# Powers ahead of other work on GpSimd, one operation for each tile's router score, and the gather split among output products

## The chip, the cores and the metric

The kernel runs on one core of one Trainium2 chip. The metric is the device time of one execution in microseconds (us); what is compared is the median of several executions.

## What is computed

One transformer layer without learned scales: attention with shared keys and values, a layer norm, a feed-forward network that only half of the rows pass through, and another layer norm. Cut to what matters:

```python
# x: (2, 512, 256) float32
k = x @ W_lat + b_lat                                  # one key and value of width 128 for all heads
q = (x @ W_d + b_d).reshape(2, 512, 16, 128)           # 16 heads
att = softmax(causal(q @ k.T / sqrt(128)))
y = (att @ k).reshape(2, 512, 16 * 128)
x1 = layernorm(x + y @ W_proj + b_proj)

scores = x1 @ router_weight + router_bias              # (2, 512)
top_scores, indices = top_k(scores, 256)               # half of the rows of each batch
selected = x1[indices]
h = gelu(selected @ w1 + b1)                           # 1024 wide
weighted = (h @ w2 + b2) * sigmoid(top_scores)
out = layernorm(x1 with weighted added at the selected rows)
```

## The kernel before

All work is laid out by hand: each engine has its own list of instructions, in a fixed order, and semaphores carry the dependencies. Products run in a split form: a float32 operand is cut into a rounded high part and a low part (what the rounding left), and `product` (L387) issues three matmuls, high by high, high by low and low by high. Whoever needs a product therefore waits for a high part (a cast, mostly on ACT) and a low part (a subtraction, on DVE or POOL).

**Attention.** There are 32 units, 16 heads of two batches, and a software pipeline over periods: in a period PE computes the scores of one unit, turns the probabilities of the unit before (`turn`, L473, three groups of exact transposes) and multiplies them with the values (`values`, L528), and adds the unit before that into the output projection (`project`, L505). For the turned probabilities ACT writes `pT_last` and `pT_hi` (`turned`, L723) and DVE writes `pT_lo` (`turned`, L891). Batch 0's norm, router and ranking are cut into pieces and put into single periods of batch 1's attention (`middle_piece`, L952, and `last_piece`, L982, on DVE, by the period numbers of L284).

**Router.** For each of four tiles of 128 rows `router_dots` (L1066) sums (row - mean) * weight into `dots` on DVE. POOL raises the variance to the power -1/2 (`inverse_deviation`, L1308), in two halves of two tiles; the variance was multiplied by 0.25 before (L1052), so this `rstd` is twice the true one, and all rows of x1 are kept doubled. `router_scores` (L1075) multiplies `dots` by `rstd` for the four tiles at once into `dots_scaled`, and then by 0.5 plus the bias into `score`. PE turns each tile's score column into a row, the same on all partitions (`turn_scores`, L547). `compare` (L1085) counts on DVE for each row whom it beats, PE sums the columns (`rank_cols`, L553), `losses` (L1102) and `ranks` (L1107) make the rank of each row. Batch 0's rows are scattered to DRAM by rank and read back; batch 1's are also gathered by PE, with a matrix of zeros and ones `sel` (`select`, L1114; `gather`, L573).

**After attention** nothing but batch 1's router chain and both networks is left. The order of each engine around the change is:
- PE (L669 to L679): the last hidden products of batch 0, two of the eight output products of rows 0 (`net_out(0, 0, ...)`), `turn_scores(1)`, the other six, `rank_cols(1)`, three products of rows 1, all of `gather`, five products, the hidden layer of batch 1, and its output products for rows 0 and rows 1. In `net_out` the argument f runs over eight slices of the hidden width; a slice is one `product`, three matmuls.
- DVE (L1148 to L1172): norm statistics, aggregates and variances of the two halves (`ps_out` holds the rows), four `router_dots`, `router_scores`, `layernorm_apply` of tiles 0 and 1, four `compare`, `losses`, `gates`, `layernorm_apply` of tiles 2 and 3, `ranks`, `select` of tiles 0 and 1, a low part, `select` of tiles 2 and 3, `layernorm_stats` of the four tiles, `chosen_low` (the low part of the gathered rows, which the hidden layer of batch 1 waits for), aggregates, variances, and `add_up` of batch 0. Then the low parts of batch 1's hidden layer (`hidden_low`, L1174), with norm work between them.
- POOL (L1357 to L1373): `hidden_low` (L1351) for the eight slices of batch 0, with the first power ahead of slice 3 and the second ahead of slice 4; `x1_low(0)` (L1315), the four scatters of `push(1)`, powers, the two scatters of batch 0's chosen rows (`put_back`, L1342), and then for each of batch 1's two row groups a power (L1371) and its scatter.
- ACT: gelu and casts; `row_of_scores(1)` (L787), `x1_high` (L782) and `chosen` (L813) come between the two hidden layers.
- SP: loads and stores, `store_all(0)`, `load_picked(1)`, `store_all(1)` (L377 to L380).

The two score operations, as they stand before:

```python
dve.tensor_tensor(dots_scaled[:, b, :], dots[:, b, :], rstd[:, b, :],
                  ALU.mult).then_inc(dots_scaled_done[b], 1)
dve.wait_ge(dots_scaled_done[b], 1)
dve.tensor_scalar(score[:, b, :], dots_scaled[:, b, :], 0.5, rb_all[:, 0:1],
                  ALU.mult, ALU.add).then_inc(score_done[b], 1)
```

## Time and profile before

| what | value |
|---|---|
| median of 3 runs | 287.74 us (287.42 to 287.77) |
| the profiled execution's own time | 287.92 us |
| its span, first to last instruction | 286.2 us |
| granted clock of PE, mean | 0.995 |
| PE busy | 275.0 us, 96% of the span |
| DVE busy | 220.6 us, 77% |
| ACT busy | 208.2 us, 73% |
| POOL busy | 155.5 us, 54% |

The span is counted from the start of the first instruction; 1.7 us of the execution's time lie around it. All points of time below are microseconds from the start of the span. Attention ends at about 253.7; the rest is the tail of the kernel. The chain of waits is the list of what ended last, step by step; the timelines list the instructions of one engine with their start and duration, and in brackets the idle time before one and who ended it. Instructions of an engine overlap a little: the next one starts some 0.08 us before the end of the one in front on DVE, and matmuls are pipelined.

### The profile page before, as it was taken

What the parts mean: (1) busy time and instruction counts of PE and PEld (TensorE: products, weight loads), DVE (VectorE), ACT (ScalarE), POOL (GpSimd) and SP (SyncE); (2) the same over time, 40 slices, a digit from 0 to 9 for tenths busy, and PEclk for the clock granted to TensorE, in tenths of its full rate; (3) what the DMA queues carried; (4) which work ended last, traced back from release to release, by engine and by line L of the source; (5) the groups of instructions that cost most, each with busy time, mean ns of one, the idle gap of its engine ahead of it and who ended that gap; (6) DMA issues with size and microseconds to landing.
All of it is one profiled execution on the core that took longest, in us unless ns stands there. A gap on an engine that the chain in (4) does not pass through costs nothing.

```text
span 286.2 us, 6205 instructions
## 1 busy us (share of the span) xinstructions
PE 275.0 (96%) x1886; PEld 249.1 (87%) x1886; DVE 220.6 (77%) x698; ACT 208.2 (73%) x571; POOL 155.5 (54%) x215
## 2 busy tenths in 40 slices
PE   7998999999999999999999999999999999998990
PEld 4777999999999999999999999998999999897990
DVE  2588777777777777777888888899978987679782
ACT  3588778777777777888897777788777777863540
POOL 3737743333333346555556756666668664257543
PEclk9999999999999999999999999999999999999998
DMA  5582111111111111111111111111112210020331
GB/s 186 128 293 76 53 32 33 33 36 37 37 37 37 37 37 40 37 37 41 37 37 39 37 40 37 38 39 37 40 38 76 58 36 2 1 76 0 99 124 37
DMA packets 18842, 15.53 MB, mean 54 GB/s; under 512 B 1641, under 2 KB 18178, under 8 KB 18818
## 3 DMA queue, kind: packets, MB, share of 16 engines
q1 hardware_dynamic: 18242, 13.65, 16.4%
q0 software_dynamic: 576, 1.58, 1.6%
q8 instruction: 12, 0.20, 0.3%
q14 instruction: 12, 0.10, 0.1%
HBM read 12.60 MB, written 2.63 MB: 53 GB/s over the span
## 4 chain that ended last, share of the span: by engine, by line
PE 83%; DVE 7%; ACT 3%; issue 2%; POOL 2%; SPq 1%; DMA 1%; POOLq 0%; DVEq 0%; ACTq 0%
PE bank L390 18%; PE bank L392 17%; PE bank L391 16%; PE bank L491 8%; PE ps_out L390 6%; PE ps_out L392 6%; PE ps_out L391 6%; PE bank L544 2%; PE bank L469 2%; DVE hid_lo L1177 1%; DMA bias_rows<-in_L_ffn_b 1%; DVE beats L1098 1%; DVE x_row L1063 1%; DVE st L1036 1%; PE bank L581 0%
## 5 line engine op out<-in xcount | busy, mean ns | idle before, releaser
L720 ACT ACTIVATE probs<-probs,negmax 128x512 f32<-128x512 f32 (+3 forms) x128 | 72.6, 575 | 6.5 <-DVE negmax L887 5.1
L1230 POOL TENSOR_TENSOR wd_hi<-wd_raw,zero 128x256 fp32r<-128x256 f32 x32 | 24.7, 772 | 92.3 <-DVE probs L948 87.5
L727 ACT CAST pT_hi<-bank 128x512 fp32r<-128x512 f32 (+2 forms) x96 | 43.5, 488 | 28.6 <-PE bank L491 28.6
L887 DVE CUSTOM_DVE_ANT_0 probs<-bank,mask_row 128x512 f32<-128x512 f32 (+3 forms) x128 | 59.1, 482 | 0.6 <-PE bank L392 0.6
L894 DVE TENSOR_TENSOR pT_lo<-bank,pT_hi 128x512 fp32r<-128x512 f32 (+2 forms) x96 | 53.0, 553 | 7.4 <-ACT pT_hi L727 6.8
L491 PEld LDWEIGHTS bank<-ident_r,prob_words 128*128 128x128 f32 x320 | 34.2, 140 | 5.6 <-issue 0.2
L390 PE MATMUL bank<-kT_hi,qT_hi 128*128 128x512 f32 (+2 forms) x96 | 37.3, 388 | 0.2 <-DVE qT_lo L841 0.2
L390 PE MATMUL ps_out<-wp_hi,yT_hi 128*128 128x256 f32 x124 | 37.2, 300 | 0.0
L392 PE MATMUL ps_out<-wp_hi,yT_lo 128*128 128x256 f32 x124 | 35.0, 282 | 0.0
L491 PE MATMUL bank<-ident_r,prob_words 128*128 128x128 f32 x320 | 35.0, 240 | 0.0
L391 PE MATMUL ps_out<-wp_lo,yT_hi 128*128 128x256 f32 x124 | 35.0, 282 | 0.0
L390 PE MATMUL bank<-pT_hi,k_hi 128*128 128x512 f32 (+2 forms) x96 | 32.9, 342 | 1.1 <-DVE pT_lo L894 1.1
L905 DVE TENSOR_TENSOR yT_lo<-bank,yT_hi 128x512 fp32r<-128x512 f32 x31 | 21.4, 690 | 16.2 <-PE bank L392 12.3
L392 PE MATMUL bank<-kT_hi,qT_lo 128*128 128x512 f32 (+2 forms) x96 | 32.6, 340 | 0.0
L391 PE MATMUL bank<-pT_lo,k_hi 128*128 128x512 f32 (+2 forms) x96 | 32.4, 337 | 0.0
L391 PE MATMUL bank<-kT_lo,qT_hi 128*128 128x512 f32 (+2 forms) x96 | 32.4, 337 | 0.0
L392 PE MATMUL bank<-pT_hi,k_lo 128*128 128x512 f32 (+2 forms) x96 | 32.2, 335 | 0.0
L948 DVE TENSOR_SCALAR probs<-probs,rinv 128x384 f32<-128x384 f32 (+2 forms) x96 | 28.7, 356 | 1.1
L769 ACT ACTIVATE probs<-probs,rinv 128x512 f32<-128x512 f32 x32 | 23.2, 724 | 8.2 <-DVE rinv L942 8.2
L1230 POOL TENSOR_TENSOR wp_hi<-wp_raw,zero 128x256 fp32r<-128x256 f32 x32 | 23.5, 736 | 10.2 <-DVE probs L948 10.2
L841 DVE SCALAR_TENSOR_TENSOR qT_lo<-bank,bias_cols,qT_hi 128x384 fp32r<-128x384 f32 x32 | 19.7, 617 | 11.8 <-ACT qT_hi L690 11.2
L390 PE MATMUL bank<-xT_hi,wd_hi 128*128 128x512 f32 x64 | 27.8, 434 | 0.1
(168 smaller groups left out, 728.7 us busy)
## 6 DMA issues: line engine op xcount, KB each, us to landing
wd_raw<-in_L_attn_W_d SPq DMA_DIRECT2D x32, 128.0 KB, 2.2
wp_raw<-in_L_attn_W_proj SPq DMA_DIRECT2D x32, 128.0 KB, 2.1
wf_raw<-in_L_ffn_w SPq DMA_DIRECT2D x2, 1024.0 KB, 7.1
x_nat<-in_L_attn_x SPq DMA_DIRECT2D x4, 256.0 KB, 2.9
out<-z_all SPq DMA_DIRECT2D x4, 256.0 KB, 2.2
picked<-ranked SPq DMA_DIRECT2D x2, 258.0 KB, 3.1
wlat_raw<-in_L_attn_W_lat SPq DMA_DIRECT2D x1, 128.0 KB, 3.5
bproj_all<-in_L_attn_b_proj SPq DMA_DIRECT2D x1, 128.0 KB, 3.4
```

The source lines that it names most:

```text
L390: pe.matmul(dst, lh, rh, start=first, stop=False, skip_group_check=check)
L391: pe.matmul(dst, lh, rl, start=False, stop=False, skip_group_check=check)
L392: return pe.matmul(dst, ll, rh, start=False, stop=last, skip_group_check=check)
L491: last = pe.transpose(dst[:, a:a + P].bitcast(F32R), prob_words[s][:, P_OFF[j] + i * P:P_OFF[j] + (i + 1) * P], ident_r[:, :])
L720: act.activation(p_tile(s, j), p_tile(s, j), ACT.Exp, bias=negmax[:, s, j:j + 1], scale=-1.0, accum_out=sums[:, s, j:j + 1]).then_inc(exp_ ...
L727: act.copy(pT_hi[:, turns[n][3]], turns[n][2]).then_inc(pt_hi_done, 1)
L769: act.mul(p_tile(at.place(0), 3), p_tile(at.place(0), 3), rinv[:, at.place(0), 3:4]).then_inc(norm_act, 1)
L887: dve.tensor_tensor_reduce(p_tile(s, j), score_bank[j], mask_row[:, (TILES - 1 - j) * P:], -SCALE, -MASKED, ALU.add, ALU.min, accum_out=ne ...
L894: dve.tensor_tensor(pT_lo[:, dst], src, pT_hi[:, dst].bitcast(F32), ALU.subtract).then_inc(pt_lo_done, 1)
L905: dve.tensor_tensor(y_lo[:, :], ps_y[:, :], y_hi[:, :].bitcast(F32), ALU.subtract).then_inc(y_lo_done, 1)
L948: dve.tensor_scalar(p_tile(s, j), p_tile(s, j), rinv[:, s, j:j + 1], None, ALU.mult).then_inc(norm_dve, 1)
L1230: pool.tensor_tensor(hi, src, nothing, ALU.add).then_inc(hi_done, 1)
```

## The change

- POOL: batch 1's second power comes right behind its first, ahead of `hidden_low(3)`; at the end both powers come ahead of both scatters of batch 1.
- DVE: the router's weight row is halved once, in period 16 (`rw_half`), and used by `router_dots`; `router_scores` becomes four operations of one column each, with two scalars per partition (`rstd` and the bias), and each counts up `score_done`.
- PE: `turn_scores` waits for one tile's score at a time and is an exact transpose of 32-bit words (the float32r form, as for the probabilities) instead of a float32 one. `gather` is cut in two halves: four products of rows 1, half the gather, one product, the other half, three products.
- In the last values period (at.fixed == UNITS, period 32) `pT_last` is copied by DVE behind its `pT_lo`, no longer by ACT ahead of `pT_hi`.
- DVE: the norm statistics of tiles 2 and 3 of batch 1 move behind `chosen_low`.

```diff
+        words = ExitStack()
+        score = sb("score", [P, BATCH, TILES], F32, words)
+        words.close()
+        score_words = sb("score_words", [P, BATCH, TILES], F32R)
+        rw_half = sb("rw_half", [P, DIM])
...
             def turn_scores(b, dst):
-                pe.wait_ge(score_done[b], 1)
                 for j in range(TILES):
-                    last = pe.transpose(dst[:, j * P:(j + 1) * P], score[:, b, j:j + 1].to_broadcast([P, P]), ident[:, :])
+                    pe.wait_ge(score_done[b], j + 1)
+                    last = pe.transpose(dst[:, j * P:(j + 1) * P].bitcast(F32R),
+                                        score_words[:, b, j:j + 1].to_broadcast([P, P]), ident_r[:, :])
...
-            def gather():
+            def gather(half):
-                pe.wait_ge(gelu_done[0], FCH)
-                for j in range(TILES):
+                if half == 0:
+                    pe.wait_ge(gelu_done[0], FCH)
+                for j in (2 * half, 2 * half + 1):
...
             rank_cols(1, ps_t1)
-            net_out(0, 1, range(0, 3))
-            gather()
-            net_out(0, 1, range(3, FCH))
+            net_out(0, 1, range(0, 4))
+            gather(0)
+            net_out(0, 1, range(4, 5))
+            gather(1)
+            net_out(0, 1, range(5, FCH))
...
             def turned(at, n):
                 wait(act, pt_ready, at.p * 3 - 2 + n)
-                if n == 2:
+                if n == 2 and at.fixed != UNITS:
                     act.copy(pT_last[:, :], ps_t0[:, 0:P]).then_inc(pt_last_done, 1)
...
             def turned(at, n):
+                if n == 2 and at.fixed == UNITS:
+                    wait(dve, y_ready, UNITS - 1)
+                    dve.tensor_copy(pT_last[:, :], ps_t0[:, 0:P]).then_inc(pt_last_done, 1)
...
             def last_piece(at):
+                if at.fixed == AT_OUT - 1:
+                    dve.wait_ge(rows_in, 64)
+                    dve.tensor_scalar(rw_half[:, :], rw_all[:, :], 0.5, None, ALU.mult).then_inc(rw_halved, 1)
...
             def router_dots(b, tiles):
-                if b == 0:
-                    dve.wait_ge(consts, CONSTS)
+                dve.wait_ge(rw_halved, 1)
...
-                                             rw_all[:, :], ALU.subtract, ALU.mult,
+                                             rw_half[:, :], ALU.subtract, ALU.mult,
...
-                dve.tensor_tensor(dots_scaled[:, b, :], dots[:, b, :], rstd[:, b, :],
-                                  ALU.mult).then_inc(dots_scaled_done[b], 1)
-                dve.wait_ge(dots_scaled_done[b], 1)
-                dve.tensor_scalar(score[:, b, :], dots_scaled[:, b, :], 0.5, rb_all[:, 0:1],
-                                  ALU.mult, ALU.add).then_inc(score_done[b], 1)
+                for j in range(TILES):
+                    dve.tensor_scalar(score[:, b, j:j + 1], dots[:, b, j:j + 1], rstd[:, b, j:j + 1], rb_all[:, 0:1],
+                                      ALU.mult, ALU.add).then_inc(score_done[b], 1)
...
             def compare(b, tiles):
+                dve.wait_ge(score_done[b], TILES)
...
-            layernorm_stats(1, 1, range(TILES))
+            layernorm_stats(1, 1, (0, 1))
             chosen_low()
+            layernorm_stats(1, 1, (2, 3))
...
             for f in range(FCH):
-                if f in (3, 4):
-                    inverse_deviation(1, 0, f - 3)
+                if f == 3:
+                    for half in range(2):
+                        inverse_deviation(1, 0, half)
                 hidden_low(f)
...
             for r in range(RCH):
                 pool.wait_ge(last_var_done, r + 1)
                 pool.tensor_tensor(rstd[:, 2 * BATCH + 1, r:r + 1], ve[:, 2 * BATCH + 1, r:r + 1],
                                    minus_half[:, r:r + 1], ALU.pow).then_inc(rstd_done[1], 1)
+            for r in range(RCH):
                 put_back(1, r)
```

## Rows read from the trace of the kernel before

**Rows 1.** Chain of waits, head 31's values: start us, us, what.
```profile
248.90 0.15 ACT pT_last L726
...
249.84 0.39 PE bank L390
```

**Rows 2.** Chain of waits, PE at batch 0's score turn.
```profile
186.28 0.44 PE bank L550 x4
...
187.95 0.56 PE bank L491 x7
```

**Rows 3.** Timeline of DVE, batch 1's scores: start us, us, instruction, [idle before].
```profile
255.27 0.17 DVE L1052 TENSOR_SCALAR ve<-mv 128x2 f32<-128x2 f32 x1
...
256.97 0.08 DVE L1071 DVE_READ_ACCUMULATOR squared<-ps_out,mv,rw_all 128x1 f32 x1
257.65 0.62 DVE L1079 TENSOR_TENSOR dots_scaled<-dots,rstd 128x4 f32<-128x4 f32 x1 [0.60 <-POOL rstd L1313]
258.31 0.65 DVE L1082 TENSOR_SCALAR score<-dots_scaled,rb_all 128x4 f32<-128x4 f32 x1
258.88 0.98 DVE L1063 TENSOR_SCALAR x_row<-ps_out,mv,rstd 128x256 f32<-128x256 f32 x2
259.78 0.73 DVE L1098 SCALAR_TENSOR_TENSOR beats<-bank,score,later 128x512 bf16<-128x512 f32 x1
...
261.78 0.16 DVE L1105 TENSOR_TENSOR lost<-behind,won 128x4 f32<-128x4 f32 x1
```

**Rows 4.** Timeline of POOL beside them.
```profile
256.86 0.68 POOL L1313 TENSOR_TENSOR rstd<-ve,minus_half 128x2 f32<-128x2 f32 x1
257.52 2.79 POOL L1354 TENSOR_TENSOR hid_lo<-hid,hid_hi 128x256 fp32r<-128x256 f32 x4
260.59 1.20 POOL L1318 TENSOR_TENSOR x_lo<-x_row,x_hi 128x512 fp32r<-128x512 f32 x1 [0.28 <-ACT x_hi L784]
```

**Rows 5.** Timelines of POOL and DVE at batch 0's scores.
```profile
183.10 0.74 POOL L1232 TENSOR_TENSOR wf_lo<-wf_raw,wf_hi 128x256 fp32r<-128x256 f32 x1
...
183.35 0.51 DVE L1079 TENSOR_TENSOR dots_scaled<-dots,rstd 128x4 f32<-128x4 f32 x1
183.89 0.23 DVE L1082 TENSOR_SCALAR score<-dots_scaled,rb_all 128x4 f32<-128x4 f32 x1
```

**Rows 6.** Timeline of DVE, two operations on one column.
```profile
278.01 0.15 DVE L1200 TENSOR_SCALAR ve<-squares 128x1 f32<-128x1 f32 x1 [0.67 <-ACT squared L834]
278.08 0.14 DVE L1205 TENSOR_SCALAR minus_mean<-z_sum 128x1 f32<-128x1 f32 x1
```

**Rows 7.** Timelines of PE, ACT and DVE from the scores to the hidden layer.
```profile
259.02 0.65 PE L550 MATMUL bank<-ident,score 128*128 128x128 f32 x4 [0.90 <-DVE score L1082]
...
263.60 0.35 PE L581 MATMUL bank<-sel,x_hi 128*128 128x256 f32 x1 [0.22 <-DVE sel L1118]
...
267.70 0.28 PE L390 MATMUL ps_out<-xs_hi,wf_hi 128*128 128x256 f32 x1
...
273.40 0.28 PE L390 MATMUL bank<-wf_hi,hid_hi 128*128 128x256 f32 x1
...
265.89 0.66 ACT L816 ACTIVATE xs_hi<-bank 128x256 fp32r<-128x256 f32 x2 [2.31 <-PE bank L583]
...
270.13 0.43 DVE L1177 TENSOR_TENSOR hid_lo<-hid,hid_hi 128x256 fp32r<-128x256 f32 x1 [1.66 <-ACT hid_hi L803]
```

**Rows 8.** Timelines of POOL and DVE at the end.
```profile
276.05 0.96 POOL L1347 DMA_INDIRECT out<-z,picked  x1 [0.30 <-issue]
...
281.13 0.58 POOL L1371 TENSOR_TENSOR rstd<-ve,minus_half 128x1 f32<-128x1 f32 x1
282.95 1.04 POOL L1347 DMA_INDIRECT out<-z,picked  x1 [1.24 <-DVE z L1211]
...
280.58 0.15 DVE L1200 TENSOR_SCALAR ve<-squares 128x1 f32<-128x1 f32 x1 [0.48 <-ACT squared L834]
281.75 0.41 DVE L1211 TENSOR_SCALAR z<-z,minus_mean,rstd 128x256 f32<-128x256 f32 x1 [1.02 <-POOL rstd L1371]
```

More of the change, by code:

```diff
@@ L110, in mk_layer_kernel @@
         dots = sb("dots", [P, BATCH, TILES])
-        score = sb("score", [P, BATCH, TILES])
+        words = ExitStack()
[3 more added lines that the diff above has]
+        rw_half = sb("rw_half", [P, DIM])
         score_row = sb("score_row", [P, SEQ])
@@ L115, in mk_layer_kernel @@
         lost = sb("lost", [P, BATCH, TILES])
-        dots_scaled = sb("dots_scaled", [P, BATCH, TILES])
         rank = sb("rank", [P, TILES])
@@ L160, in mk_layer_kernel @@
             sems(n) for n in ("stats_done", "aggr_done", "var_done", "rstd_done", "ln_done"))
-        dots_done, dots_scaled_done, score_done, score_turned, score_row_done = (
-            sems(n) for n in ("dots_done", "dots_scaled_done", "score_done", "score_turned", "score_row_done"))
+        dots_done, score_done, score_turned, score_row_done = (
+            sems(n) for n in ("dots_done", "score_done", "score_turned", "score_row_done"))
+        rw_halved = sem("rw_halved")
         lost_done = sems("lost_done")
```

## The prediction

> **What bounds the kernel now.** I read the chain of waits first. Through attention it is almost all PE, back to back, so a PE instruction that gets shorter there is time gained, and so is the one place where the chain leaves PE: in period 32 PE waits for the last low part, and `pT_last` on ACT is a link of 0.15 us of that wait [rows 1]. Batch 0's score turn is itself on the chain, with 0.44 us for four transposes, where seven of the float32r form take 0.56 [rows 2].
>
> Then the timelines of the tail, from 253.7 on, engine by engine. PE has work enough there but stands in front of two things: 0.90 us before the score transposes and 0.22 before the gather [rows 7]. What it waits for is a chain over DVE and POOL. DVE has the second variance ready at 255.44 (255.27 + 0.17) and the last dot product at 257.05 [rows 3]. POOL's second power stands behind `hidden_low(3)`, which waits for ACT, and runs from 256.86 to 257.54 [rows 4]. The two score operations then take until 258.96, two norm operations run, `compare` starts at 259.78 and `losses` at 261.78 [rows 3]; the gather starts at 263.60 and batch 1's hidden layer at 267.70 [rows 7]. From there PE is the bound again: 48 matmuls in 273.40 - 267.70 = 5.70 us, 0.119 each, with no idle time up to the end of the products [rows 7]. Behind them comes a short chain over DVE, ACT and POOL to the last scatter at 282.95 [rows 8]. So the question is by how much the hidden layer of batch 1 starts earlier, and what the end gives or takes.
>
> **The score operations and POOL.** They have four elements per partition and should take 0.2 us, but took 0.62 and 0.65 [rows 3]. The four `hidden_low` run back to back from 257.52 to 260.31, 0.70 us apart, so they end near 258.22 and 258.93 [rows 4]; the two DVE operations end at 258.27 and 258.96. For batch 0 it is the same: the first took 0.51 and ended at 183.86, where a subtraction of POOL ended at 183.84; the second met an idle POOL and took 0.23 [rows 5]. I read this as one lock: a DVE operation with two SBUF inputs, or a `tensor_scalar` from SBUF to SBUF on four columns, waits until POOL's running operation is done. The norm operations beside the same `hidden_low` read PSUM and show no such stretch (0.98 for two) [rows 3].
>
> After the change there are four `tensor_scalar` of one column each. Their price is the unknown of this case, since no one-column operation of the trace runs beside a POOL `tensor_tensor`. The cheap end: they don't use the lock, and go 0.07 us apart and 0.15 long [rows 6], 3 x 0.07 + 0.15 = 0.36 for all. The dear end: each waits for one `hidden_low`, four times 0.70. I take the cheap end, by the nearest rows in form, but those stood beside an idle POOL, so this is a choice, not a reading. The Trainium skill bears on it: its page "SBUF — State Buffer", section "Who interferes with whom", has the port pair that DVE and GpSimd share as an exclusive lock, held for a whole instruction, which the trace's ends agree with. The Trainium skill's "Advanced Engine Details and Errata", under "2x-2p Requirements", wants the outermost non-unit dimension even or odd and above one for the mode that takes the second port, and by this one column stays free of the lock; the sum by it is the one below. The Trainium skill's "Vector Engine (DVE) Microarchitecture Reference", section 5.1, leaves "above one" out; by that the first rival would come true, at its 287.7. No row here decides between the two pages.
>
> **From the variances to the gather**, in the times of before. POOL's second power, 0.68 long, comes straight after 255.44, when the first is long done: about 255.5 to 256.2. The five `hidden_low` follow at 0.70, to 259.7 (0.6 earlier than before). DVE is through with the dots at 257.05, so scores from 257.08 to 257.44, 1.5 us earlier than 258.96. The norms of tiles 0 and 1 follow, 257.37 to 258.3. PE is free for the transposes at 259.02 - 0.90 = 258.12 [rows 7]; four of them at 0.08 [rows 2] plus some 0.1 of latency end at 258.5. So `compare` starts at 258.5 instead of 259.78, now held by PE, and ends at 260.5. `losses` has two SBUF inputs: it comes at 260.5 while POOL runs `x1_low(0)`, from 259.74 for 1.20 us [rows 4]; this is the wait that is late next. It ends at 260.97 instead of 261.94, and what follows on DVE up to `select` is the same work with an idle POOL. **The gather starts 0.9 us earlier**, at 262.7. For half the scores' gain the lock is paid once more.
>
> PE until then: six products, 18 x 0.119 = 2.14, from 258.45 to 260.6; `rank_cols` 0.3 behind `compare`, to 260.9; four products, 1.43, to 262.35. It still waits 0.35 us for `sel`.
>
> **From the gather to the hidden layer.** Before, 16 gather matmuls and five products (15 matmuls) took 4.10 us, 263.60 to 267.70 [rows 7]: 31 x 0.119 = 3.69 and 0.4 of gaps, most of it where the gather waited for the third tile of `sel`. After, 16 and 12 matmuls, 28 x 0.119 = 3.33, and one product stands where PE waited for the third tile. Start at 266.05: **another 0.75 us**, of which I count 0.7. The cover: ACT's high part began 2.29 us after the gather's start [rows 7] and now does so at about 265.0; high and low part of the first half are there at 265.8, of the second at 266.1, needed at 266.05 and 0.36 later. It holds, because the statistics of tiles 2 and 3 no longer stand ahead of the low parts. With them in front it would fail by some 0.3. DVE was idle for 1.66 us before the first low part of batch 1's hidden layer [rows 7]; its list comes 0.9 earlier and is due 1.6 earlier, and 0.5 is lost waiting for ACT, so 0.3 to 0.4 of idle time stays.
>
> **The end.** Before, the second group's variance was there at 280.73, but POOL's scatter of the first ran until its power at 281.13; then the norm, and the last scatter at 282.95 [rows 8]. After (same clock): power 280.8 to 281.4, scatter of the first at + 0.30, the gap between scatters that wait for nothing [rows 8], 281.7 to 282.74, the last at 283.04. The 0.4 us that the power gains is given back by the scatter that now stands in the way: **+0.1**. Bounds: -0.3 if the first scatter hides in the norm's time, +0.5 if a scatter behind a power needs the whole gap of 0.79 that the last one had behind the norm (from 281.75 + 0.41 = 282.16 to 282.95).
>
> **Small parts.** `pT_last` off ACT: high part, low part and PE come 0.15 us earlier; DVE's copy of 128 columns, 0.28 by the nearest, begins behind the low part and ends before PE has done its next three matmuls (0.36). It pushes DVE's four norms of batch 0 back, which had that much idle time behind them: **-0.15**, bounds 0 and -0.2. Float32r transposes for batch 0: four at 0.08 against 0.44, **-0.12**, all PE's, bounds 0 and -0.2. `rw_half`: one `tensor_scalar` in period 16 behind the last norm of the probabilities, where DVE then waits for PE: 0; if POOL's split holds it 0.7 longer, up to 0.2. The extra waits on one score each stop PE's products for under 0.1, as all four come within 0.3.
>
> **Sum:** -0.15 - 0.12 - 0.9 - 0.7 + 0.1 = -1.8 us. The profiled execution took 287.92 and would take 286.1; the median, 287.74, lies 0.18 below it, so **286.0**. A difference of 0.2%, 0.58 us, is about what a measurement of this kernel tells from none.
>
> **Rivals.**
> - *One column takes the lock too, and waits for one `hidden_low` each.* Scores end at 257.67, 258.37, 259.07, 259.77, later than 258.96 by 0.8. For it: the rows of four columns. Against: in the trace nothing, since the case isn't there. The gather starts 0.8 later, at 264.4, PE has its four products ready by then and regains 0.7 in the order: +0.8 - 0.7 - 0.27 + 0.1 = -0.1, **287.7**.
> - *The lock costs both ways* (the slower side). Place: the same four operations. If POOL's next `hidden_low` also starts late by the DVE operation's own time, 0.2 us, the four take 4 x 0.9 and end at 260.5: +1.5 - 0.7 - 0.27 + 0.1 = +0.6, **288.3**. It decides from the point where the scores end after 259.8, which is what the rest can pay for. Against it: the `hidden_low` of before kept their 0.70 spacing with DVE operations between them [rows 4].
> - *The scores are free, but the end keeps part of it.* The scatter costs its dear bound, 0.5, and DVE or the gathered rows come 0.3 late for batch 1's hidden layer: -1.8 + 0.4 + 0.3 = -1.1, **286.6**.
> - *The earlier power does nothing,* as POOL's second power waits for something else than `hidden_low(3)`: the timeline names only ACT in front of it; this is the weakest, and would give 0.5 less than the forecast at most.
>
> **Chances.** Forecast 0.57, kept-back end 0.16, one-column lock 0.17, lock both ways 0.07, else 0.03. The first two are faster by over 0.2% with few exceptions: 0.72. The plain lock is within 0.2%: with some of the others 0.20. Slower 0.08. The likeliest case alone gives 285.4 to 286.7; for eight in ten the range must reach the plain lock: 285.3 to 287.7.
>
> **What would show it.** Scores in the timeline of DVE: four operations 0.07 apart beside `hidden_low` (forecast), or 0.7 apart (rivals). `compare` starts right behind the last transpose; `losses` is stretched to the end of `x1_low(0)`. PE idles under 0.4 us before the first gather matmul, none between the halves. Gather to hidden layer 3.3 to 3.4 us. At the end power, scatter, scatter on POOL without waits. The prediction is wrong if the scores end after 258.5, or if the time from the hidden layer's start to the end grows by more than 0.3.

## The result, and the profile after

The changed kernel takes 285.83 us (median of 6 runs), against 287.66 for the kernel before, measured beside it. The ratio is 0.9931, with an interval from 0.9913 to 0.995: faster by 1.8 us. The forecast was 286.0. The profiled execution took 285.84 us, against 287.92 for the one profiled before: the spans are 284.1 and 286.2 us, the mean granted clocks 0.992 and 0.995 of full speed. So the two profiles differ by 2.1 us, somewhat more than the medians do.

The tail falls into stretches whose ends are single instructions. Each time is the difference of two starts in the timelines; "statistics" is DVE's first operation on batch 1's projected rows, "gather" PE's first gather matmul, "hidden layer" its first matmul for batch 1's hidden layer, and "last product" its last matmul.

| stretch | before | after | difference | forecast |
|---|---|---|---|---|
| start of the span to the statistics | 253.18 | 252.66 | -0.52 | -0.27 |
| statistics to the gather on PE | 10.42 | 9.40 | -1.02 | -0.9 |
| gather to batch 1's hidden layer | 4.10 | 3.40 | -0.70 | -0.7 |
| hidden layer to the last product | 11.34 | 11.54 | +0.20 | 0 |
| last product to the last scatter | 3.91 | 3.94 | +0.03 | +0.1 |
| last scatter to the end | 3.25 | 3.16 | -0.09 | 0 |

**Before the statistics.** The chain of waits in head 31's period (start us, us, what; it answers to [rows 1]) no longer has a `pT_last`:

```profile
248.56 0.27 ACT pT_hi L735
...
248.85 0.44 DVE pT_lo L902
...
249.33 0.39 PE bank L394
```

The high part comes straight behind `gelu_first`. PE's timeline at batch 0's score turn, in the kernel before:

```profile
185.77 0.28 PE L392 MATMUL bank<-pT_hi,k_lo 128*128 128x256 f32 x1
...
186.78 0.39 PE L391 MATMUL bank<-kT_lo,qT_hi 128*128 128x512 f32 x1
```

and in the changed one:

```profile
185.56 0.28 PE L396 MATMUL bank<-pT_hi,k_lo 128*128 128x256 f32 x1
...
185.81 0.52 PE L554 MATMUL bank<-ident_r,score_words 128*128 128x128 f32 x4
...
186.47 0.39 PE L395 MATMUL bank<-kT_lo,qT_hi 128*128 128x512 f32 x1
```

From the last matmul ahead of the turn to the second one behind it, PE takes 0.91 us for the same list of products instead of 1.01, so the other form of the four transposes gains 0.10. (In the chain of waits they take 0.28 instead of 0.44 [rows 2], but the matmul behind them takes 0.30 instead of 0.23.) Of the 0.52 us, 0.24 is neither this nor `pT_last`: near 60 us, ahead of everything that the change touches, DVE's reciprocal of the sums already starts at 60.17 instead of 60.41. In the other traces of this document it lies between 60.08 and 60.46, and some 2 us later in two of them, so such a difference comes with the execution.

**The scores.** DVE's timeline, batch 1 (columns as in [rows 3], to which it answers):

```profile
256.58 0.82 DVE L1094 TENSOR_SCALAR score<-dots,rstd,rb_all 128x1 f32<-128x1 f32 x4
257.31 0.99 DVE L1078 TENSOR_SCALAR x_row<-ps_out,mv,rstd 128x256 f32<-128x256 f32 x2
258.21 0.74 DVE L1111 SCALAR_TENSOR_TENSOR beats<-bank,score,later 128x512 bf16<-128x512 f32 x1
...
260.22 0.20 DVE L1118 TENSOR_TENSOR lost<-behind,won 128x4 f32<-128x4 f32 x1
```

POOL beside it ([rows 4] before):

```profile
255.06 0.69 POOL L1327 TENSOR_TENSOR rstd<-ve,minus_half 128x2 f32<-128x2 f32 x1 [0.36 <-DVE ve L1067]
255.72 3.52 POOL L1368 TENSOR_TENSOR hid_lo<-hid,hid_hi 128x256 fp32r<-128x256 f32 x5
259.20 1.20 POOL L1332 TENSOR_TENSOR x_lo<-x_row,x_hi 128x512 fp32r<-128x512 f32 x1
```

POOL's second power starts at 255.06 behind the first, and DVE finds both powers done when its last dot product ends at 256.54: no idle time before `score`, where 0.60 stood. Four score operations run from 256.58 to 257.40 while `hidden_low` runs all the time, and none of them stretches to the end of one: each takes 0.27, 0.18 apart. `losses` (`lost`) arrives at 260.22, and POOL's `x1_low(0)` ends at 260.40.

**Gather and hidden layer.** PE, ACT and DVE ([rows 7] before):

```profile
257.48 0.44 PE L554 MATMUL bank<-ident_r,score_words 128*128 128x128 f32 x4
...
262.06 0.36 PE L587 MATMUL bank<-sel,x_hi 128*128 128x256 f32 x1
...
263.44 0.28 PE L587 MATMUL bank<-sel,x_hi 128*128 128x256 f32 x1
...
265.46 0.28 PE L394 MATMUL ps_out<-xs_hi,wf_hi 128*128 128x256 f32 x1
...
264.36 0.66 ACT L824 ACTIVATE xs_hi<-bank 128x256 fp32r<-128x256 f32 x2 [2.31 <-PE bank L589]
...
267.84 0.47 ACT L806 ACTIVATE hid<-ps_out,bias_cols 128x256 f32<-128x256 f32 x1 [0.98 <-PE bank L396]
...
264.78 0.76 DVE L1147 SCALAR_TENSOR_TENSOR xs_lo<-bank,xs_hi 128x256 fp32r<-128x256 f32 x2 [0.64 <-ACT xs_hi L824]
```

PE hardly waits before the first gather matmul any more (0.06 us, from the spacing of its matmuls; 0.22 before), and the second half at 263.44 stands behind one product instead of behind a wait. The low parts of the gathered rows (264.78) are there before PE asks for them at 265.46. One thing is new: the second gelu of batch 1 starts at 267.84, after 0.98 us of idle time, where before it came 0.71 behind the first.

**The end**, POOL and then DVE ([rows 8] before):

```profile
278.85 0.55 POOL L1386 TENSOR_TENSOR rstd<-ve,minus_half 128x1 f32<-128x1 f32 x1 [1.75 <-DVE ve L1214]
279.59 1.04 POOL L1361 DMA_INDIRECT out<-z,picked  x1 [0.18 <-issue]
280.94 0.96 POOL L1361 DMA_INDIRECT out<-z,picked  x1 [0.30 <-issue]
...
279.44 0.47 DVE L1225 TENSOR_SCALAR z<-z,minus_mean,rstd 128x256 f32<-128x256 f32 x1 [0.67 <-POOL rstd L1386]
```

Power, scatter, scatter: the first scatter starts 0.18 behind the power, the second 0.30 behind the first, and the norm (279.44 to 279.91) lies under the first scatter.

### The profile page after: what moved, and what is told of

Read it like the earlier page. It is cut to its first block, busy times and chain, and to the rows that moved or that the text cites. A ratio compares the mean times of both kernels' runs of the same rounds, so it can differ in the third digit from the quotient of the medians.

```text
span 284.1 us, 6215 instructions
## 1 busy us (share of the span) xinstructions
PE 274.3 (97%) x1886; PEld 248.6 (87%) x1886; DVE 220.4 (78%) x704; ACT 207.8 (73%) x570; POOL 155.2 (55%) x215
## 4 chain that ended last, share of the span: by engine, by line
PE 85%; DVE 4%; ACT 4%; issue 3%; SPq 1%; DMA 1%; POOL 1%; POOLq 1%; ACTq 0%; DVEq 0%
PE bank L394 18%; PE bank L396 17%; PE bank L395 17%; PE bank L495 8%; PE ps_out L394 6%; PE ps_out L396 6%; PE ps_out L395 6%; PE bank L548 2%; PE bank L473 2%; ACT hid L806 1%; DMA bias_rows<-in_L_ffn_b 1%; DVE beats L1111 1%; DVE squared L1085 1%; POOLq L60 1%; DVE st L1051 1%
```

## The experiments

Each edit is against the changed kernel unless it says otherwise. Runs of one set shared a chip and its runs of the kernel before, whose median was 287.53, 287.59 and 287.53 in the three sets. The first set holds the two old operations, the powers among the low parts, the gather in one piece and the power between the scatters; the second the changed kernel again, the statistics and the two last kernels; the third the other four. The changed kernel itself ran in none but the second set. Where a median is compared with it, both its values are used, 285.83 from the first measurement and 285.58 from that set. They lie 0.25 us apart, so a difference of that size between sets tells nothing, and the traces carry the argument there.

### The changed kernel again

No edit.

> The changed kernel itself, to stand beside the others on this chip: 285.8 us by every theory, and the second gelu of batch 1's hidden layer again about 0.7 us behind its products, as in its first trace (267.84), if that is no accident of one execution.

Measured: 285.58 us, ratio 0.9933 [0.9911, 0.9956], 2.0 us less than the kernel before. The gain stands in a second measurement. Here the second gelu isn't late, against what was expected (ACT's timeline, same columns):

```profile
267.29 0.48 ACT L806 ACTIVATE hid<-ps_out,bias_cols 128x256 f32<-128x256 f32 x1 [0.24 <-PE ps_out L396]
```

It comes 0.72 behind the first, and hidden layer to last product takes 11.33 us, as before the change (11.34). So the +0.20 of the table belongs to that execution and not to the edit.

### The two old score operations

```diff
-                for j in range(TILES):
-                    dve.tensor_scalar(score[:, b, j:j + 1], dots[:, b, j:j + 1], rstd[:, b, j:j + 1], rb_all[:, 0:1],
-                                      ALU.mult, ALU.add).then_inc(score_done[b], 1)
+                dve.tensor_tensor(dots_scaled[:, b, :], dots[:, b, :], rstd[:, b, :],
+                                  ALU.mult).then_inc(dots_scaled_done[b], 1)
+                dve.wait_ge(dots_scaled_done[b], 1)
+                dve.tensor_scalar(score[:, b, :], dots_scaled[:, b, :], 1.0, rb_all[:, 0:1],
+                                  ALU.mult, ALU.add).then_inc(score_done[b], 1)
```

> The changed kernel with the two score operations of four columns as before (two SBUF inputs, then a tensor_scalar on four columns); the halved weights, the early power and all else stay. Lock theory (four columns wait for POOL's running operation, one column doesn't): in the changed kernel's clock the first operation comes at 256.58 and ends with hidden_low at about 257.1, the second ends with the next one at about 257.8, where the four single ones ended at 257.40; norms, compare and gather come 0.4 later, the time rises by 0.4 us to about 286.2. Rival, the count of operations is what matters: two operations at 0.16 and 0.23 us end 0.3 us earlier than four at 0.18, and the time falls by up to 0.3, to 285.5.

Measured: 286.04 us, ratio 0.9941 [0.9919, 0.9962]. DVE, then POOL:

```profile
256.62 0.60 DVE L1095 TENSOR_TENSOR dots_scaled<-dots,rstd 128x4 f32<-128x4 f32 x1
257.25 0.67 DVE L1098 TENSOR_SCALAR score<-dots_scaled,rb_all 128x4 f32<-128x4 f32 x1
...
255.77 3.52 POOL L1372 TENSOR_TENSOR hid_lo<-hid,hid_hi 128x256 fp32r<-128x256 f32 x5
```

POOL's five low parts are 0.70 apart, so they end near 256.5, 257.2 and 257.9. The two operations end at 257.22 and 257.92, each with one low part: the lock that the prediction read out of [rows 3] and [rows 5] is shown, since only the form of the operations differs (and PE waits once for all four scores). The gather then starts 9.85 us behind the statistics, 0.45 later than with one-column operations. The medians differ by 0.2 to 0.5, with intervals that overlap.

### Each power where it was, among the low parts

```diff
-                if f == 3:
-                    for half in range(2):
-                        inverse_deviation(1, 0, half)
+                if f in (3, 4):
+                    inverse_deviation(1, 0, f - 3)
```

> The changed kernel with batch 1's second power behind hidden_low(3) again. Lock and chain theory: the power runs from about 256.35 to 257.03, so the scores start at 257.06 instead of 256.58; 0.4 to 0.5 us slower, about 286.3. Rival, the early power does nothing because the scores were held by something else: no difference, 285.8.

Measured: 286.31 us, ratio 0.9953 [0.9937, 0.997], 0.5 to 0.7 us over the changed kernel. POOL:

```profile
255.59 0.73 POOL L1368 TENSOR_TENSOR hid_lo<-hid,hid_hi 128x256 fp32r<-128x256 f32 x1 [0.95 <-ACT hid_hi L811]
256.29 0.69 POOL L1327 TENSOR_TENSOR rstd<-ve,minus_half 128x2 f32<-128x2 f32 x1
```

The second power again stands behind a low part that waited 0.95 us for ACT. DVE's scores wait for it and start at 257.09 instead of 256.58, and the gather comes 9.98 us behind the statistics instead of 9.40. The 0.58 us is more than half of what the stretch gained.

### The one-column scores alone, in the kernel before

The same four operations and `rw_half`, put into the kernel before, with everything else as it was there; PE waits for all four scores at once.

```diff
+                for j in range(TILES):
+                    dve.tensor_scalar(score[:, b, j:j + 1], dots[:, b, j:j + 1], rstd[:, b, j:j + 1], rb_all[:, 0:1],
+                                      ALU.mult, ALU.add).then_inc(score_done[b], 1)
```

> The kernel before with the four one-column score operations alone (and the halved weights they need). Scores from 257.65 to 258.47 in its clock instead of 258.96, compare 0.5 earlier at 259.28; x1_low(0) then runs from 260.3 to 261.5, and losses, at 261.3, waits for it: what is left is 0.4 us, about 287.2 against 287.6. Rival, the time is set by PE's pauses and not by this chain: no difference. Rival by the prediction's price for four operations (0.36): 0.8 faster.

Measured: 287.29 us, ratio 0.9987 [0.9965, 1.0009]; the median doesn't tell it from none. The trace does: scores from 257.62 to 258.36 (0.82 for all, 0.27 each), gather at 263.11 instead of 263.60. Against the statistics (253.13 here) that is 0.44 us. With the 0.58 of the power it makes up the 1.02 of the table.

### One scalar operand per score operation

The bias moves into the argument of the tanh, so a score operation reads one scalar from SBUF instead of two. A bias that is the same for all rows changes no rank.

```diff
-                    dve.tensor_scalar(score[:, b, j:j + 1], dots[:, b, j:j + 1], rstd[:, b, j:j + 1], rb_all[:, 0:1],
-                                      ALU.mult, ALU.add).then_inc(score_done[b], 1)
+                    dve.tensor_scalar(score[:, b, j:j + 1], dots[:, b, j:j + 1], rstd[:, b, j:j + 1], None,
+                                      ALU.mult).then_inc(score_done[b], 1)
```

> The changed kernel with one scalar less in each score operation: the router's bias, which is the same for all rows and leaves the ranking alone, is added ahead of tanh by ACT instead. The prediction's step under test: scores of 0.36 us and a losses that waits for x1_low(0). Scores take 0.36 instead of 0.82, compare starts 0.4 earlier, and losses, now at 259.8 in the changed kernel's clock, waits until x1_low(0) ends at 260.4: the gain is given back to within 0.1, 285.6 where the changed kernel is at 285.6 to 285.7. Rival, the lock doesn't hold losses: 0.4 faster.

Measured: 285.36 us, ratio 0.9919 [0.9893, 0.9945]. DVE, then POOL:

```profile
256.27 0.58 DVE L1096 TENSOR_SCALAR score<-dots,rstd 128x1 f32<-128x1 f32 x4
...
257.67 0.74 DVE L1113 SCALAR_TENSOR_TENSOR beats<-bank,score,later 128x512 bf16<-128x512 f32 x1
...
259.66 0.45 DVE L1120 TENSOR_TENSOR lost<-behind,won 128x4 f32<-128x4 f32 x1
...
258.89 1.21 POOL L1334 TENSOR_TENSOR x_lo<-x_row,x_hi 128x512 fp32r<-128x512 f32 x1
```

The four take 0.58 instead of 0.82, not the 0.36 expected: one operation is 0.21 long and 0.12 from the next. `compare` starts 5.32 us behind the statistics (252.35 here) instead of 5.55. `losses` now arrives at 259.66 and takes 0.45, to 260.11, where `x1_low(0)` ends at 260.10; without POOL beside it the same operation takes 0.16 to 0.20. The gather starts 9.41 us behind the statistics, as in the changed kernel (9.40). What the scores gained is given back whole at the next lock. The median is lower than the changed kernel's by 0.2 to 0.5, with intervals that overlap. By the traces the edit has no part in that: from the statistics on, all stretches are those of the repeated run (the hidden layer to the last product takes 11.34 against 11.33). Ahead of them this execution leads the repeated run by 0.16 us at the reciprocal (60.12 against 60.28) and by 0.48 at the statistics (252.35 against 252.83), and the lead grows evenly through attention, to 0.41 before batch 0's scores are turned. Where it comes from was not looked into.

### Operations of one, two, three and four columns beside POOL

A probe whose time of the whole means nothing. Fourteen additions are put on POOL, back to back, and on DVE rows of small operations ahead of the scores: `tensor_scalar` with a constant (L1106), with two scalars from SBUF (L1108), `tensor_tensor` (L1110).

```diff
+            def probe():
+                dve.wait_ge(rstd_done[1], 2)
+                dve.wait_ge(consts, CONSTS)
+                at = 0
+                for n, times, form in ((1, 3, "imm"), (2, 2, "imm"), (1, 3, "imm"), (3, 2, "imm"), (1, 3, "ptr"), (4, 2, "imm"), (1, 2, "tt"), (1, 3, "imm")):
...
+                    for n in range(14):
+                        pool.tensor_tensor(wf_raw[:, n * DIM:(n + 1) * DIM], zero[:, 0:DIM], zero[:, DIM:2 * DIM], ALU.add)
```

> A measurement in the changed kernel: 14 additions of 256 columns, of no use otherwise, run on POOL ahead of hidden_low(3), and beside them DVE does 3 tensor_scalar of one column, 2 of two, 3 of one, 2 of three, 3 of one with two scalars from SBUF, 2 of four, 2 tensor_tensor of one column, 3 tensor_scalar of one. The time of the kernel says nothing. Lock theory, with one column free: the one-column tensor_scalar go 0.07 to 0.08 us apart and are 0.15 long, those with two SBUF scalars 0.18 apart and 0.27 long whatever POOL does; those of two, three and four columns and the tensor_tensor end with an operation of POOL each, up to 0.7 us. Rival, the lock is taken for even counts only: three columns go free as well. Rival, the number of scalars and not POOL makes an operation slow: none is longer than 0.3.

DVE's timeline in narrow stretches, so that each form stands by itself, then POOL's additions:

```profile
256.52 0.27 DVE L1106 TENSOR_SCALAR probe_dst<-zero 128x1 f32<-128x1 f32 x3
256.71 0.61 DVE L1106 TENSOR_SCALAR probe_dst<-zero 128x2 f32<-128x2 f32 x2
...
257.42 0.52 DVE L1106 TENSOR_SCALAR probe_dst<-zero 128x3 f32<-128x3 f32 x1
...
257.93 0.62 DVE L1108 TENSOR_SCALAR probe_dst<-zero,minus_half 128x1 f32<-128x1 f32 x3
258.47 0.22 DVE L1106 TENSOR_SCALAR probe_dst<-zero 128x4 f32<-128x4 f32 x2
258.61 0.75 DVE L1110 TENSOR_TENSOR probe_dst<-zero,minus_half 128x1 f32<-128x1 f32 x2
...
255.79 9.63 POOL L1394 TENSOR_TENSOR wf_raw<-zero 128x256 f32<-128x256 f32 x14
```

The additions start 0.69 apart, so they end near 256.48, 257.16, 257.85, 258.54 and 259.22. One column with a constant: 0.15 us each, 0.07 apart, in the middle of an addition. Two columns: the first starts at 256.71 and the pair ends only at 257.32, behind 257.16. Three columns: the first takes 0.52, from 257.42 to 257.94, behind 257.85. One column with two scalars: 0.26 each, 0.18 apart, not held at 257.85 to 258.54. Four columns: the pair (258.47, 0.22) stood just at the boundary of 258.54 and shows nothing; the run with the two old operations does, with 0.67. `tensor_tensor`, one column: 0.68, to 259.29, held. So a `tensor_tensor` with two inputs from SBUF takes the lock at one column as at four, and a `tensor_scalar` from SBUF to SBUF is free of it at one column and takes it at two, three and four. For the `tensor_scalar` the Trainium skill's "Advanced Engine Details and Errata" has these widths under "2x-2p Requirements" (even, or odd and above one), as the condition of the mode that takes the second port; the held operations of two and three columns and the free ones of one column agree. The Trainium skill's "Vector Engine (DVE) Microarchitecture Reference", section 5.1, leaves out "above one", and by it one column would be held too; the 0.15 us here do not agree. And the 0.27 us of a score operation are no lock but the price of the scalar operands from SBUF. POOL was at work in both cases, and the second arithmetic operation is not it either: with two constants, a multiplication and an addition on one column take 0.15 us as well (`ve` in [rows 6]). By the run above, one such scalar makes it 0.21.

### The gather in one piece

```diff
-            net_out(0, 1, range(0, 4))
+            net_out(0, 1, range(0, 3))
             gather(0)
-            net_out(0, 1, range(4, 5))
             gather(1)
-            net_out(0, 1, range(5, FCH))
+            net_out(0, 1, range(3, FCH))
```

> The changed kernel with three products, the whole gather, five products, as before; the statistics of tiles 2 and 3 stay behind the low parts. My theory: the gather's start stays, PE waits 0.3 for the third tile of sel, and gather to hidden layer is 4.0 to 4.1 us instead of 3.40: 0.6 to 0.7 slower, about 286.5. Rival, PE's order only moves idle time to another place: within 0.1 of the changed kernel.

Measured: 286.22 us, ratio 0.9948 [0.9929, 0.9966], 0.4 to 0.6 over the changed kernel. PE:

```profile
262.08 0.36 PE L587 MATMUL bank<-sel,x_hi 128*128 128x256 f32 x1 [0.26 <-DVE sel L1130]
...
266.19 0.28 PE L394 MATMUL ps_out<-xs_hi,wf_hi 128*128 128x256 f32 x1
```

Gather to hidden layer takes 4.11 us, as before the change (4.10), against 3.40. PE waits 0.26 for `sel` with three products ahead of it. The gather starts 9.41 us behind the statistics, as in the changed kernel (9.40), so the whole 0.7 is the order, as forecast.

### Statistics of tiles 2 and 3 back ahead of the low parts

```diff
-            layernorm_stats(1, 1, (0, 1))
+            layernorm_stats(1, 1, range(TILES))
             chosen_low()
-            layernorm_stats(1, 1, (2, 3))
```

> The changed kernel with the norm statistics of all four tiles ahead of the low parts again. By the prediction the low part of the second half would then come 0.3 us late for the hidden layer. By the trace of the changed kernel DVE was idle for 0.64 us ahead of the first low part, and two statistics take 0.67, so they should just fit: no difference to within 0.1 (285.8), 0.2 slower at most.

Measured: 285.67 us, ratio 0.9926 [0.9903, 0.9949], beside 285.58 for the changed kernel in the same set: no difference. DVE:

```profile
263.52 1.39 DVE L1051 BATCH_NORM_STATS2 st<-x_row 128x6 f32<-128x256 f32 x4
264.89 0.76 DVE L1147 SCALAR_TENSOR_TENSOR xs_lo<-bank,xs_hi 128x256 fp32r<-128x256 f32 x2
```

The four statistics now fill what was 0.64 us of idle time, and the low parts start as early as in the changed kernel, in both traces 12.12 us behind the statistics of batch 1's projected rows. PE asks for the first at 265.57 and gets it. This part of the change gains nothing. It even leaves less slack later: ahead of the first low part of batch 1's hidden layer DVE is idle for 1.06 us here and for 0.42 us in the repeated run.

### `pT_last` back on ACT

```diff
-                if n == 2 and at.fixed != UNITS:
+                if n == 2:
                     act.copy(pT_last[:, :], ps_t0[:, 0:P]).then_inc(pt_last_done, 1)
```

The copy on DVE is taken out.

> The changed kernel with pT_last of period 32 on ACT again. Theory: 0.15 us slower, 285.8 where the changed kernel itself is at 285.6 to 285.8; in the trace the pause of PE ahead of the last values product is 0.15 longer. Rival, the copy on DVE cost as much elsewhere: no difference.

Measured: 285.82 us, ratio 0.993 [0.9908, 0.9953], which the medians don't tell from the changed kernel. DVE:

```profile
250.68 0.42 DVE L902 TENSOR_TENSOR pT_lo<-bank,pT_hi 128x256 fp32r<-128x256 f32 x1 [1.17 <-ACT pT_hi L735]
```

DVE's idle time ahead of that low part is 1.17 us with the copy on ACT and 1.00 in both traces of the changed kernel: 0.17 us, small and where it was expected. PE's matmuls around the wait are 0.60 apart instead of 0.42.

### The second power back between the scatters

```diff
             for r in range(RCH):
                 pool.wait_ge(last_var_done, r + 1)
                 pool.tensor_tensor(rstd[:, 2 * BATCH + 1, r:r + 1], ve[:, 2 * BATCH + 1, r:r + 1],
                                    minus_half[:, r:r + 1], ALU.pow).then_inc(rstd_done[1], 1)
-            for r in range(RCH):
                 put_back(1, r)
```

> The changed kernel with the end in the old order on POOL: power, scatter, power, scatter. My theory (the scatter in the way takes back what the power gains): add_up of the second group to the last scatter goes from 3.48 to 3.5 to 3.75 us; 0 to 0.3 slower, 285.9 to 286.1. Rival, the earlier power is worth its whole wait: 0.4 or more slower, from 286.2.

Measured: 286.16 us, ratio 0.9948 [0.9928, 0.9967], 0.3 to 0.6 over the changed kernel, and between the two expectations (up to 286.1, from 286.2). POOL:

```profile
278.29 1.04 POOL L1361 DMA_INDIRECT out<-z,picked  x1 [1.24 <-DVE z L1225]
279.36 0.58 POOL L1386 TENSOR_TENSOR rstd<-ve,minus_half 128x1 f32<-128x1 f32 x1
281.18 1.04 POOL L1361 DMA_INDIRECT out<-z,picked  x1 [1.24 <-DVE z L1225]
```

Last product to last scatter takes 4.23 us, against 3.94. The kernel before has the same order and takes only 3.91, since its two variances are 2.57 us apart [rows 6, 8]. Here they are 2.33 apart (276.24 and 278.57), and 2.34 in the changed kernel's profile, both with the late gelu; and the first scatter, which follows the first variance by the same 2.05, stands 0.24 longer in front of the second power. So how much the new order saves hangs on that spacing: 0.3 us here, and 0.1 at a spacing of 2.5 (3.99 in the kernel before with one-column scores, 3.87 in the repeated run). What counts is the gap in front of a scatter that has just waited for the norm: `z` ends at 280.39, the scatter starts at 281.18, 0.79 later, as before. Scatters that wait for nothing start after 0.18 and 0.30.

### Old order at the end, the norm's wait first

`put_back` waits for two things, the norm and the store of the rows, and the norm always comes last. Only the order of the two waits is turned, on top of the edit above.

```diff
-                pool.wait_ge(stored[b], 32)
                 pool.wait_ge(ln_done[b], 2 * TILES + r + 1)
+                pool.wait_ge(stored[b], 32)
```

> The changed kernel with the end in the old order (power, scatter, power, scatter) and, in put_back, the wait for the norm ahead of the wait for the stores, so that the wait that comes true last no longer stands right ahead of the scatter. Theory W: the 0.79 us between a norm's end and its scatter is the price of waiting at the scatter itself, and falls to the 0.3 us that push shows behind rank_no; then the first scatter is done 0.5 earlier, the second power doesn't wait for it, and the last scatter comes about 0.8 us earlier than in the changed kernel: 285.0. Rival, the gap is the scatter's own preparation after any wait: like the run with the power between the scatters, about 0.3 slower than the changed kernel, 286.1.

Measured: 284.99 us, ratio 0.9903 [0.988, 0.9926]: 0.6 under the changed kernel of the same set, and 1.2 under the edit above, which was in another set. DVE and POOL (this trace lies some 2 us later as a whole: the matmuls of PE's first products, from 8.1 to 10.7 us, are 0.43 us apart, where the repeated run has 0.23, at a granted clock of 1.00 in both):

```profile
281.35 0.41 DVE L1225 TENSOR_SCALAR z<-z,minus_mean,rstd 128x256 f32<-128x256 f32 x1 [0.70 <-POOL rstd L1386]
...
282.05 1.04 POOL L1361 DMA_INDIRECT out<-z,picked  x1 [0.74 <-DVE z L1225]
```

The norm ends at 281.76 and the scatter starts at 282.05: 0.29 instead of 0.79. Last product to last scatter takes 3.11 us. So the 0.79 was not the scatter's own price behind a norm. By this pair of runs it is paid when the wait that is met last stands directly ahead of the scatter, and not when another, already met, stands between them. The changed kernel has a scatter of the second kind already: `push` waits for the ranks first, then for things long done, and its first scatter starts at 261.95, 0.28 behind the end of `rank_no` (261.67).

### The last root on ACT and DVE, waits in the good order

The last deviations are no power on POOL: ACT takes the root straight behind its sum of squares, DVE the reciprocal. A first root while ACT is idle brings its table in. The waits are as in the run before.

```diff
+            act.activation(sqrt_first[:, :], eps_all[:, 0:1], ACT.Sqrt)
...
+                act.wait_ge(squares_done, r + 1)
+                act.activation(ve[:, 2 * BATCH + 1, r:r + 1], squares[:, r:r + 1], ACT.Sqrt, bias=eps_all[:, 0:1],
+                               scale=1.0 / DIM ** 3).then_inc(last_var_done, 1)
...
+                dve.wait_ge(last_var_done, r + 1)
+                dve.reciprocal(rstd[:, 2 * BATCH + 1, r:r + 1], ve[:, 2 * BATCH + 1, r:r + 1]).then_inc(rstd_done[1], 1)
```

> The changed kernel with the last inverse deviations by ACT (square root, its table loaded while ACT is idle) and DVE (reciprocal) instead of DVE and POOL, and the two waits of put_back in the other order. It leaves no part of the computation out. If the chain behind the last product is what ends the kernel: the norm of the second group ends 0.4 us earlier, POOL is free for both scatters, and by theory W the last one starts 0.3 behind the norm, 1.1 to 1.2 earlier than in the changed kernel: 284.7. Without W: 0.7 earlier, 285.1. Rival, the square root's table is loaded again between the groups: 1.3 slower than that.

Measured: 284.28 us, ratio 0.9878 [0.9855, 0.9901]: 1.3 under the changed kernel of the same set, the fastest here and 0.4 under what was expected. ACT, DVE and POOL:

```profile
272.37 1.28 ACT L839 ACT_TABLE_LOAD   x1
...
278.16 0.29 ACT L847 ACTIVATE ve<-squares,eps_all 128x1 f32<-128x1 f32 x1
...
278.49 0.16 DVE L1219 RECIPROCAL rstd<-ve 128x1 f32<-128x1 f32 x1 [0.81 <-ACT ve L847]
278.69 0.41 DVE L1229 TENSOR_SCALAR z<-z,minus_mean,rstd 128x256 f32<-128x256 f32 x1
...
279.38 0.96 POOL L1366 DMA_INDIRECT out<-z,picked  x1 [1.32 <-DVE z L1229]
```

The table takes 1.28 us, in a stretch where ACT has nothing to do. Last product to last scatter takes 2.76 us instead of 3.87 in the repeated run: 1.1 of the 1.3 us. Of the rest, 0.27 lies ahead of the statistics already, 0.20 of it at the first reciprocal (60.08 against 60.28), and is not the edit's.

## Why the prediction was right

The forecast, scores free of the lock and no case of the rivals, came true: -1.8 us forecast, -1.8 in the medians and -2.0 in the repeated run, 286.0 forecast and 285.83 measured. Its steps one by one:

1. **`pT_last` off ACT**, -0.15: measured -0.17, by the idle time of 1.17 and 1.00. Right.
2. **Float32r transposes of batch 0**, -0.12: measured -0.10, from the two timelines; it was not undone by itself. Right.
3. **POOL's power straight behind the variance**: right. Taking it back costs 0.58 us up to the gather and 0.5 to 0.7 in the median.
4. **One column takes no lock**: right, where the prediction could only choose. The probe shows it apart from everything else.
5. **0.36 us for four score operations: the mis-sized term.** They took 0.82. The prediction took its price from [rows 6], operations with constants and without scalars from SBUF. With two such scalars an operation is 0.27 long and 0.18 from the next. The scores end 4.74 us behind the statistics, not 4.26.
6. **`compare` held by PE**: wrong in its holder. With the scores 0.46 later the last norm operation, ending at 258.21 to 258.30, is what it follows; the transposes were done by 257.92. It starts at 5.55, forecast 5.32.
7. **The lock is paid once more at `losses`**, some 0.5 us: right in place, and it repaired step 5. `losses` came at 260.22, 0.18 before `x1_low(0)` ended, and ran 0.20, about 0.04 more than where nothing holds it. Its end was forecast 7.79 us behind the statistics and is 7.76. The two errors cancel for a reason: both paths end at the end of `x1_low(0)`. The run with one scalar shows it, with scores 0.24 shorter, `losses` held for the rest and the gather at 9.41 instead of 9.40. What sets the gather after the change is POOL's `x1_low(0)`; the scores have nothing left to give.
8. **0.35 us of idle time on PE before the gather**: it was 0.06. With three products the wait is 0.26, the fourth fills it. PE's own list now comes out at the same time as `sel`.
9. **0.7 us from the order of gather and products**: right, 4.11 against 3.40 by undoing it alone.
10. **"With them in front it would fail by some 0.3"** (the statistics of tiles 2 and 3): wrong. They fit into DVE's idle time of 0.64 us. The 0.3 to 0.4 us of idle time that the forecast left DVE ahead of batch 1's first low part are 0.42 in the repeated run.
11. **The end, +0.1**: +0.03 in the profile and -0.04 in the repeated run (3.87). Its parts were a scatter 0.18 behind the power, where 0.30 was taken, and two scatters in a row. The dear bound, 0.79 behind a power, did not come. The sum was against the kernel before; undone alone, the edit is worth 0.3 us, because the variances lie closer together there, behind a late gelu; at the usual spacing it is worth 0.1.

Of the trace's -0.52 ahead of the statistics, against -0.27, 0.24 is start-up and not the change. The +0.20 behind the hidden layer is the late gelu, and not the change either. In the profiles they cancel to within 0.04, which is luck; neither was foreseen. In the medians, what belongs to single executions should weigh less, but no run tells it closer than the 1.8 and 2.0 us of the two measurements.

Of the rivals, the lock on one column is excluded by the probe and by the timeline, the lock both ways by POOL's spacing of 0.70 us, which held, and the earlier power that does nothing by the run that takes it back. "The end keeps part of it" did not come: the low parts of the gathered rows were in time.

## What to carry to other kernels

Ask of every small DVE operation beside a busy POOL whether it takes two inputs from SBUF, or goes from SBUF to SBUF on more than one column: such an operation costs the rest of POOL's instruction, 0.5 to 0.7 us here, and split into single columns with scalar operands it costs 0.21 to 0.27 us and 0.12 to 0.18 for each further column. When a chain gets shorter, look for the next operation that meets the same lock, since it will take the gain until POOL's own instruction ends earlier. And where an engine waits for several semaphores ahead of an indirect DMA, try the one that comes last first; the runs here show it for scatters on POOL alone.

## What had not been expected

- **The order of two waits is worth 0.5 us per scatter.** 0.79 from the norm's end to the scatter where its wait stands directly ahead, 0.28 or 0.29 where a wait already met stands between. This gave 0.6 us against the changed kernel, although its order at the end was undone. Why was not looked into.
- **Scalars from SBUF make a one-column operation longer**: 0.15 us with a constant, 0.26 to 0.27 with two scalars, spacing 0.07 and 0.18. With one scalar it is 0.21 and the spacing 0.12.
- **The second gelu of batch 1 comes some 0.6 to 0.75 us late in some profiled executions**: in that of the changed kernel and in three of the four of the first set (in the fourth, the gather in one piece, it is the first gelu that comes 0.5 late), and in none that was timed in the two later sets, which ran on other chips, the changed kernel itself among them. From the hidden layer to the last product the four traces with a late second gelu take 11.38 to 11.54 us, those without 11.24 to 11.34, so it costs 0.2 us in the changed kernel's first profile and some 0.1 or less in the other three. What causes it stays open, and was not tried.
